# Wider transfers, a gather through SBUF, and the scores of two units as two steps

## The chip, the cores and the metric

The kernel runs on one core of one Trainium2 chip. The metric is the time of one execution in device microseconds (us). The kernel before took 1416.16 us (median of three runs, 1413.11 to 1417.28); lower is better.

## What is computed

The input x has 4 x 1024 tokens of 128 numbers. Four layers follow one another; each works on a normalised copy and adds its result to x (up to constants, as the reference writes them):

```
Q, K, V = h@wq+bq, h@wk+bk, h@wv+bv         # h = norm(x); reshaped to (4*16, 1024, 8)
attn    = softmax(Q K^T / sqrt(8))           # 64 heads, 1024 x 1024 each
y       = norm(attn V reshaped @ wo + bo + h) * gamma + beta
h2      = silu(x@W1) * (x@W2); gelu; gelu    # ternary weights, 128 -> 512 -> 512 -> 512 -> 128
gla     : h = h*exp(g) + k v^T along the sequence; o = q h; gated, projected
moe     : a router picks 3 of 8 zones per batch; gelu(x@Wa[z])@Wb[z], weighted
```

The reshape to (4*16, 1024, 8) takes a head from 64 consecutive tokens over all 128 columns, so Q, K and the result of the attention change their layout between the projection and the scores. The kernel does this through DRAM.

## The kernel before, in words

Tokens are worked on in 8 blocks of 512 (`NBLK`). The attention of a block is 8 heads, taken as 4 pairs, so there are 32 pairs. A pair is 16 units; a unit is 128 keys of one head of the pair against its 1024 queries: two score matmuls (`scores`), one exponential over 128 x 1024 on ScalarE (line 929), and two matmuls with the values (`weigh`, four column groups of 32, line 1466, 8 records for two units). So there are 512 exponentials.

The other layers are cut into small steps that stand between the scores. `class Plan` has a generator for each kind of work (`stream_x` the scores, `stream_l` the loads of pairs, `stream_f` the fetches of results, `stream_q` norm, projection and split of Q and K, `stream_a` the attention's end, `stream_w` weights, `stream_b` the ternary layer, `stream_p`, `stream_r`, `stream_s`, `stream_t` the recurrent layer, `stream_z`, `stream_d` the zones). The string `ORDER` names, letter by letter, which generator takes its next step. Each engine plays its part of this one list strictly in order, with semaphores between engines. SyncE (SP) issues every DMA of the loop, so its queue too is in the order of the list. Unit numbers below are given as pairs: 11.44 is 0.44 of the way through the scores of pair 11.

The steps that matter on SP:

- `keep(b, w, n0, n1)` (line 682) writes the two rounded parts of Q or K of block b to the DRAM tensor QD. A block takes 8 DMAs of 64 KB each for Q and as many for K, in rows of 256 bytes.
- `load_pair(n)` (lines 698 and 707) reads the keys (4 DMAs of 128 KB) and queries (8 DMAs of 32 KB) of a pair into one of three buffers, 786 KB in all. It waits for the kept parts and for the scores of pair n - 3.
- `finish(pr)` (line 760) writes the result of a pair (DVE's copy OS, line 1220) to OD in 4 DMAs, and DVE's next copy waits for them.
- `fetch(pr)` (line 771) reads the numerators and denominators back, 4 DMAs. After four fetches DVE divides (lines 1155 and 1157) and TensorE projects (`project`, line 1478).
- `replica` (line 791) reads one row set of the recurrent layer's values, 16 per block; DVE's `product` (1267) waits for it, its scan (1276) follows.

PSUM has 8 banks. From pair 6 on (`LATE`) banks 0 to 3 are two slots of scores, bank 4 sums the pair's result, banks 5 and 6 are for all other steps in turn (`take`), and bank 7 sums `gather`: four groups of matmuls that pick the outputs of 16 states of a block into one bank, which ScalarE's `heads` then reads. `log_exp`, `tables` and `tanh_with` load another set of function tables on ScalarE (line 901) when the next function isn't in the loaded set; 135 such changes lie in the order.

Of the kernel before, what the change touches and what calls it, by code (L numbers as in the profile page):

```python
# [18 lines left out]
NS = 6  # L19
# [6 lines left out]
    "qqqxwqxxwxxxxwwxxxxxxxxxxxxxwlxxxxxxxxxxxxxwxxxqxxwxxxwxxxxfwxlxxfwxxxxwxxxxlxwxqxwxxxxwlxxxxxfxxxxx"  # L26
    "fawxxxxqwxwxxxxwfxxaxaxxaaxxxxxxwxxxwaxxxwxaxpxxwxwxxxqxwbxlqbbxxqbxxbxbbxxqxbbxxxlqxxxbxlxfbbbbxbfx"
    "lbxxbxbbfxabxbxbxbxxqxabxxxbxaxqxxpaxpxxlrqppxxxxxpxpxxraassaxxxxsrbbxxxqpxssxsxssrxxssxxrxsxsxfrsxx"
    "xsssxsbxxbsrxqxxbrsbsxxrxqslssxxfxsxrssxfxsxbblsxlxbsssxxbbbxrsxbrbxsbrsrbfbxsssxbsbxbbxsxsssabbxxxx"
    "aabxxqxssrraaxxxsqbxsxspsfxxpaxsxxrpqrxxpsqpxpxxaxsxsxsbxpxxsssbxbxsrsxlqxxsxxxrxsxsxsxrsrbbxtbxxlqs"  # L30
    "sssxfbbssxsbrlxrxxtxrtsxqbtsxrxslbbsxsxbxtssbbbxsfssxbssstxxxrbxtxbbxxbxfrasxxsbbssxsxrrsxxslxsaxbss"
    "ssxxsxrrbqsxxxpaxprsxsxsqaxpxxsxpsprpxxsssspxxstssraxxsxqrrxsxftxtaxqxaxsxtrxsbxtsxtbbsbxsfxqssxsbbx"
    "xxsssxxtxbftlrsrbxxsslxxblsxrxbstbbrxsxsfssbbsbqasbsxxbsrxsrxxxxassxasbxxbbxrsxssbaqaxsxtlxbsbrxtxxs"
    "xssfbsxxarbrtxasxxxtbbbbbxspxxxsqxsprxxrpxsxppxttsqxpfsxsssxpsxxbsstrxxsrqsrtxtxxqxsxbxsssxsxxxsbrxs"
    "xxbssssrxbsflxsxbrsbssbbsxbxbrlxlbsxrtsxsbsssxsbbxrrsfsssxtasxbtrxsxssbsxbratsxsxxsxxsbxaxqtxxbrxxxx"
    "aptsxpqsxasxqxxxafprrsqxqxprxsxaxpxxpsxsbxxxssxxsspxsxtfsrlsxxxtxrqbxtbbxstxxssrsxsxrsxtsssbxtxslssr"
    "sbrxslxrsxsfxsrsbxssstxxbsxbslxssxtxbrbxxbbsbxxbrbsrfxxbtsxbssbsxsbrsbtsaxxsbxbxxssaxbxsxxbxarxasplx"
    "xsarstxpxasxxsrpxptfxxxpxpxsrsssxabxxspxfxxstsbxsxxtrssxtxxrxxxrssxsbbxtbsssrtstsxxbsxxxssxtrssrxssr"
    "xxbrfssxsbxxbstxstbxssbsbsbzbfrbbdrdzbtrbsbssassssbsbdrzbbdatdsdadstadsdsbsddbrdsddrtapsdpptssdrazdd"
    "srdpppabdsdsssddbspdbssdddsbrddbrdzbdsdbbrsssbdtsddrdssdststbsbsbssrbbbrbbrstdsssdtbsdrsssbstsstdbsb"  # L40
# [43 lines left out]
class Plan:  # L84
# [57 lines left out]
    def norm_in(self, b):  # L142
        n = self.stats("q", "X", b, ("x_in%d" % b, 16))
        after = [("y_sum", b - 1)] if b >= 2 else []
        return self.apply("q", "XN", "X", b, n, *after)
# [58 lines left out]
    def stream_q(self):  # L204

        for b in range(1, NBLK):
            n = self.stats("q", "X", b, ("x_in%d" % b, 16))
            yield
            after = [("y_sum", b - 1)] if b >= 2 else []
# [199 lines left out]
    def stream_s(self):  # L409


        for n in range(16 * NBLK + 2):
# [8 lines left out]
            if n >= 5 and n % 4 == 1:  # L421
                m = (n - 5) // 4
                assert self.acc >= LATE
                self.add("gather", m // 4, m % 4)
                yield
# [47 lines left out]
x4_in qh gather_ps heads mean_ps rms inv_rms tanh_c swish gate_o scaled_o out_c_ps x3 xt4_ps xt4 pooled route_ps route_act logits_r  # L473
# [3 lines left out]
def build(nc, io, out):  # L477
    ctx = ExitStack()
    with ctx:
# [178 lines left out]
        def _(sp):  # L658
# [19 lines left out]
            def keep(b, w, n0, n1):  # L678
                need.wait_ge("qk_parts", split_no(b, w))
                for n in range(n0, n1):  # L680
                    for i in range(2):
                        sp.dma_start(bass.AP(QD.tensor, QD[w, b, n, i, 0, 0:1].offset, [[64, 16], [2048, 8], [1024, 2], [1, 64]]),  # L682
                                     words(Qp[w][:, i, 128 * n:128 * n + 128])).then_inc(S[kept(b, n, w)], 16)

            def load_pair(n):
                b, i4, k = n // 4, n % 4, n % 3
                need.wait_ge(kept(b, i4, 1), 128 * b + 96 if n else 64)
# [3 lines left out]
                need.wait_ge(kept(b, i4, 0), 128 * b + 96 if n else 64)  # L691
# [29 lines left out]
            def guard(b):  # L721
# [3 lines left out]
                with sp.If_eq(flag, 1):  # L725
                    inner = need.inner()
                    g_dve, g_in = "g_dve%d" % b, "g_in%d" % b
                    for n in range(3):
                        inner.wait_ge("pair_in%d" % ((4 * b + n) % 3), 192 * ((4 * b + n) // 3 + 1))
                    need_kept = ("k_out" if b else "k_out", 128 * b + 96)  # L730
                    inner.wait_ge(*need_kept)
                    inner.wait_ge("q_out", 128 * b + 96)
# [9 lines left out]
                    inner.wait_ge(g_in, 384 + 32)  # L742
# [9 lines left out]
                    inner.wait_ge(g_in, 384 + 32 + 64)  # L752

            def finish(pr):
                b, q = pr // 4, pr % 4
                need.wait_ge("ctx_copied", pr + 1)
                for gg in range(2):
                    for h in range(2):
                        c = 32 * (2 * gg + h)
                        sp.dma_start(bass.AP(OD.tensor, OD[b, q, h, 0, 0, 0, gg, 0:1].offset,  # L760
                                             [[128, 16], [2048, 8], [1, 64]]),
                                     OS[c:c + 16, :]).then_inc(S["ctx_out"], 16)

# [940 lines left out]
```

## Time and profile before

| | us |
|---|---|
| median of three runs | 1416.16 |
| the profiled execution | 1411.4 |
| its span | 1409.6 |
| TensorE busy (mean granted clock 0.862) | 1034.7 |
| ScalarE busy | 885.7 |
| of it the 512 exponentials | 489.8 |
| of it 136 table loads | 174.5 |
| VectorE busy | 686.8 |
| GpSimd busy | 348.6 |

Engines work at the same time, so their times don't add up to the span. Busy shares are averages over two very different stretches: while the attention runs (to about 1147 us) no engine is busy all the time; after it TensorE nearly is.

### The profile page before, as it was taken

The page shows a single profiled execution, that of the slowest core. Times are in us where ns is not written, and L with a number is a line of the kernel's source. Part 1 is how long each engine was busy: PE and PEld are TensorE (multiplying, and loading weights), DVE is VectorE, ACT ScalarE, POOL GpSimd, SP SyncE. Part 2 cuts the span into 40 slices and gives each one's busy share as a digit, 9 for nine tenths or more (in the row PEclk, how much of TensorE's full clock was granted, in tenths as well). Part 3 has the DMA queues.
Part 4 walks back from the last instruction along what each step waited for, and adds up shares of the span by engine and source line. Part 5 has one row for each costly group of instructions (what it writes and reads, how often), then busy time and mean ns, then how long its engine had stood idle before and what let it go on. Part 6 is the DMA issues. An engine that isn't in the chain of part 4 may idle for free.

```text
span 1409.6 us, 16763 instructions
## 1 busy us (share of the span) xinstructions
PE 1034.7 (73%) x5842; PEld 470.4 (33%) x5842; DVE 686.8 (49%) x1235; ACT 885.7 (63%) x1110; POOL 348.6 (25%) x318
## 2 busy tenths in 40 slices
PE   2755588567746956868567977495488789999998
PEld 1211123322223212412233223121152247665666
DVE  3022264053616733656355652763254669979510
ACT  0744579656845955758458876385387876665552
POOL 1000011011302302342223232221132254545300
PEclk7877789878877987998778998797688799999999
DMA  4132112102211222113121221131211123222220
GB/s 106 62 93 78 62 50 61 60 23 69 75 63 40 72 73 69 65 64 79 60 69 53 55 72 65 46 87 56 74 60 58 51 73 97 83 90 98 68 60 16
DMA packets 111423, 93.52 MB, mean 66 GB/s; under 512 B 59184, under 2 KB 82512, under 8 KB 111312
## 3 DMA queue, kind: packets, MB, share of 16 engines
q1 hardware_dynamic: 111168, 92.06, 21.6%
q8 instruction: 67, 1.10, 0.3%
q14 instruction: 44, 0.36, 0.1%
q10 hardware_dynamic: 144, 0.00, 0.0%
HBM read 75.25 MB, written 16.78 MB: 65 GB/s over the span
## 4 chain that ended last, share of the span: by engine, by line
SPq 31%; PE 22%; DMA 16%; DVE 13%; issue 9%; ACT 7%; POOL 3%; ACTq 0%; DVEq 0%; POOLq 0%
SPq L707 15%; DMA R<-VD 10%; SPq L698 6%; PE PS L1466 4%; SPq L682 4%; ACT R L929 4%; PE PS L1626 4%; PE PS L1614 4%; DVE R L1276 3%; PE PS L1443 3%; PE PS L1498 3%; DMA RA<-QD 2%; DVE R L1267 2%; SPq L771 2%; ACT L901 2%
## 5 line engine op out<-in xcount | busy, mean ns | idle before, releaser
L929 ACT ACTIVATE R<-PS 128x1024 f32<-128x1024 f32 x512 | 489.8, 1034 | 248.8 <-PE PS L1443 247.1
L1466 PE MATMUL PS<-R 128*32 128x512 f32 x2048 | 318.4, 669 | 27.4 <-DVE R L1220 27.2
L1443 PE MATMUL PS<-RA 32*128 32x512 f32 x1024 | 186.7, 547 | 137.3 <-DMA RA<-QD 58.3
L882 POOL TENSOR_TENSOR R<-R 128x512 f32<-128x512 f32 x128 | 186.3, 1462 | 301.5 <-ACT R L1004 179.9
L1498 PE MATMUL PS<-RB,WR 128*128 128x512 f32 x640 | 193.3, 443 | 59.0 <-DVE RB L1232 33.4
L1267 DVE TENSOR_TENSOR R<-R 128x512 f32<-128x512 f32 x128 | 103.8, 811 | 262.0 <-DMA R<-VD 257.9
L901 ACT ACT_TABLE_LOAD x136 | 174.5, 1283 | 47.2 <-PE PS L1498 32.1
L1443 PEld LDWEIGHTS PS<-RA 32*128 32x128 f32 x1024 | 72.0, 199 | 380.8 <-ACT R L929 188.1
L1276 DVE TENSOR_TENSOR_SCAN R<-R 128x512 f32<-128x512 f32 x128 | 191.5, 1496 | 2.6
L1498 PEld LDWEIGHTS PS<-RB,WR 128*128 128x128 f32 x640 | 123.5, 202 | 126.9 <-issue 36.1
L868 POOL TENSOR_TENSOR RB<-R,RB 128x512 fp32r<-128x512 f32 x48 | 74.1, 1544 | 278.2 <-DVE RB L1232 257.8
L1626 PEld LDWEIGHTS PS<-R 128*128 128x128 f32 x768 | 97.3, 192 | 38.0 <-issue 35.0
L1053 ACT ACTIVATE R<-PS 128x512 f32<-128x512 f32 x96 | 56.5, 596 | 75.5 <-PE PS L1614 75.4
L1626 PE MATMUL PS<-R 128*128 128x128 f32 x768 | 99.7, 276 | 2.2 <-ACT R L1062 2.0
L1614 PE MATMUL PS<-XT,R 128*128 128x512 f32 x192 | 96.4, 595 | 0.7 <-DMA R<-in_Wb 0.7
L1466 PEld LDWEIGHTS PS<-R 128*32 128x32 f32 x2048 | 48.3, 114 | 133.7 <-issue 90.9
L841 POOL TENSOR_SCALAR rs<-mv 128x4 f32<-128x4 f32 x40 | 15.2, 381 | 268.1 <-DVE mv L1092 260.8
L1570 PE MATMUL PS<-R,hot 128*32 128x512 f32 x256 | 52.5, 677 | 28.0 <-POOL R L882 27.9
L1155 DVE RECIPROCAL R<-R 128x512 f32<-128x512 f32 x8 | 26.7, 3342 | 63.1 <-DMA R<-OD 63.0
L1478 PE MATMUL PS<-wA,R 128*128 128x128 f32 x64 | 11.9, 343 | 58.6 <-DVE R L1284 21.4
L945 ACT ACTIVATE R<-PS,sB 128x512 f32<-128x512 f32 x64 | 42.4, 687 | 18.9 <-PE PS L1498 18.5
L1186 DVE CAST WR<-R 128x512 fp32r<-128x512 f32 x10 | 4.2, 421 | 88.9 <-DMA R<-in_wB 88.9
(121 smaller groups left out, 903.2 us busy)
## 6 DMA issues: line engine op xcount, KB each, us to landing
R<-VD SPq DMA_DIRECT2D x128, 256.0 KB
RA<-QD SPq DMA_DIRECT2D x128, 128.0 KB
QD<-RA SPq DMA_DIRECT2D x128, 64.0 KB, 2.1
RA<-QD SPq DMA_DIRECT2D x256, 32.0 KB
OD<-R SPq DMA_DIRECT2D x128, 32.0 KB, 1.8
R<-OD SPq DMA_DIRECT2D x128, 32.0 KB
R<-in_Wa SPq DMA_DIRECT2D x12, 256.0 KB, 3.5
R<-in_Wb SPq DMA_DIRECT2D x12, 256.0 KB, 4.0
```

What stands on the lines that cost most here:

```text
L698: sp.dma_start(words(KS[k][p:p + 32, :]), bass.AP(QD.tensor, QD[1, n // 4, n % 4, 0, 0, 1024 * gg:1024 * gg + 1].offset, [[0, 2], [2048, 1 ...
L707: sp.dma_start(words(QS[k][p:p + 16, :]), bass.AP(QD.tensor, QD[0, n // 4, n % 4, i, 0, at:at + 1].offset, [[0, 2], [2048, 8], [1, 512]])) ...
L882: pool.tensor_tensor(st, st, Qc, ALU.mult).then_inc(S["qh"], 1)
L901: act.preload_act_table_set(name)
L929: act.activation(PR[u % 4], bank(2 * s, 1024), ACT.Exp, scale=SC).then_inc(S["exp"], 1)
L1267: dve.tensor_tensor(ST[n % NS], ST[n % NS], Kc, ALU.mult).then_inc(S["kv"], 1)
L1276: dve.tensor_tensor_scan(st, Ac, st, CS[:, v:v + 1] if k else 0.0, ALU.mult, ALU.add).then_inc(S["scanned"], 1)
L1443: op = pe.matmul(bank(2 * s + h), exact(KS[k][p:p + 32, 128 * j:128 * j + 128]), exact(QS[k][p:p + 32, :]), start=True, stop=not guarded[0])
L1466: op = pe.matmul(bank(ob)[c:c + 32, :], VAF[b % 2][:, at:at + 32], PR[u % 4][:, 512 * h:512 * h + 512], start=(j == 0), stop=(j == 7), til ...
L1498: return pe.matmul(out_ap, w, x, **kw)
L1614: pe.matmul(bank(bk), WA[r][:, 128 * m:128 * m + 128], xtblock(b), start=True, stop=True).then_inc(S["zone_up_ps"], 1)
L1626: op = pe.matmul(bank(bk)[:, 128 * i:128 * i + 128], HH[t % NH][:, 128 * i:128 * i + 128], WB[r][:, m % 4, :], start=(m == 0 and i == 0), ...
```

## The change

Five edits, of which the first three change transfers:

1. QD and OD are laid out anew. The columns of wq, wk and their biases and the rows of wo are permuted on the host, so that a pair is loaded by two DMAs (keys 512 KB, queries 256 KB) in place of twelve. `keep` writes each part twice: 4 DMAs for a call in place of 2 for each of its pairs; for a whole block 4 of 256 KB in place of 8 of 64 KB, still in rows of 256 bytes.
2. `finish` is one DMA of 128 partitions of 2 KB in place of 4.
3. `fetch` is still 4 DMAs with the same bytes, but now of 64 partitions over two halves of OD, in rows of 256 bytes in place of 512.
4. `gather` takes a bank from the common turn for each of its four groups, and VectorE copies or adds it into a tile GA (in the place of Y2), which `heads` reads. Bank 7 joins banks 5 and 6 in the turn.
5. `stream_x` yields between the scores of unit u and of unit u + 1. ORDER is new: 769 letters x in place of 513, all others in the same number, at other places. The residual's tile Y2 is gone (XN is used), so a norm waits for `x1` and not `y_sum`.

```diff
-    "qqqxwqxxwxxxxwwxxxxxxxxxxxxxwlxxxxxxxxxxxxxwxxxqxxwxxxwxxxxfwxlxxfwxxxxwxxxxlxwxqxwxxxxwlxxxxxfxxxxx"
...
+    "xxxxqxxxxxxqxxxxxxxxxxqxxxxxwxqxxxfxxwxxxxxlxwxxxxxxxxxxxxxxxxxxqxxxxxxxxxxxxxfxxxxxxxxxxxxxxxxwxqxw"
...
-        banks = ((5, 6) if self.acc < 32 else
-                 {"b": (0, 1, 2), "d": (0, 1, 2), "o": (3, 4), "a": (4,), "c": (5, 6)}[who])
+        banks = ((5, 6, 7) if self.acc < 32 else
+                 {"b": (0, 1, 2), "d": (0, 1, 2), "o": (3, 4), "a": (4,), "c": (5, 6, 7)}[who])
...
                 self.add("scores", u)
                 yield
+                self.add("scores", u + 1)
+                yield
...
-                for n in range(n0, n1):
-                    for i in range(2):
-                        sp.dma_start(bass.AP(QD.tensor, QD[w, b, n, i, 0, 0:1].offset, [[64, 16], [2048, 8], [1024, 2], [1, 64]]),
-                                     words(Qp[w][:, i, 128 * n:128 * n + 128])).then_inc(S[kept(b, n, w)], 16)
+                for i in range(2):
+                    for copy in range(2):
+                        at = 2 * copy + i if w else 2 * i + copy
+                        sp.dma_start(bass.AP(QD.tensor, QD[w, b, 2 * n0, at, 0, 0:1].offset,
+                                             [[64, 128], [32768, 2 * (n1 - n0)], [1, 64]]),
+                                     words(Qp[w][:, i, 128 * n0:128 * n1])).then_inc(S[kept(b, n0, w)], 16)
...
             def keys(n, k, landed):
-                for h in range(2):
-                    for gg in range(2):
-                        p = 32 * (2 * h + gg)
-                        sp.dma_start(words(KS[k][p:p + 32, :]),
-                                     bass.AP(QD.tensor, QD[1, n // 4, n % 4, 0, 0, 1024 * gg:1024 * gg + 1].offset,
-                                             [[0, 2], [2048, 16], [1, 1024]])).then_inc(S[landed], 16)
+                sp.dma_start(words(KS[k][:, :]), bass.AP(QD.tensor, QD[1, n // 4, 2 * (n % 4), 0, 0, 0:1].offset,
+                                                         [[0, 2], [1024, 64], [1, 1024]])).then_inc(S[landed], 16)
 
             def queries(n, k, landed):
-                for h in range(2):
-                    for gg in range(2):
-                        for i in range(2):
-                            p, at = 32 * (2 * h + gg) + 16 * i, 1024 * gg + 512 * h
-                            sp.dma_start(words(QS[k][p:p + 16, :]),
-                                         bass.AP(QD.tensor, QD[0, n // 4, n % 4, i, 0, at:at + 1].offset,
-                                                 [[0, 2], [2048, 8], [1, 512]])).then_inc(S[landed], 16)
+                sp.dma_start(words(QS[k][:, :]), bass.AP(QD.tensor, QD[0, n // 4, 2 * (n % 4), 0, 0, 0:1].offset,
+                                                         [[512, 2], [1024, 64], [1, 512]])).then_inc(S[landed], 16)
...
             def finish(pr):
...
-                for gg in range(2):
-                    for h in range(2):
-                        c = 32 * (2 * gg + h)
-                        sp.dma_start(bass.AP(OD.tensor, OD[b, q, h, 0, 0, 0, gg, 0:1].offset,
-                                             [[128, 16], [2048, 8], [1, 64]]),
-                                     OS[c:c + 16, :]).then_inc(S["ctx_out"], 16)
+                sp.dma_start(OD[b, q, :, :], OS).then_inc(S["ctx_out"], 16)
 
             def fetch(pr):
...
-                for h in range(2):
-                    for n, dst in enumerate((CT, DT)):
-                        sp.dma_start(dst[b % 2][64 * h:64 * h + 64, 128 * q:128 * q + 128],
-                                     bass.AP(OD.tensor, OD[b, q, h, 0, n, 0, 0, 0:1].offset,
-                                             [[2048, 8], [128, 8], [1, 128]])).then_inc(S["ctx_in%d" % (b % 2)], 16)
+                for n, dst in enumerate((CT, DT)):
+                    for gg in range(2):
+                        at = 128 * q + 64 * gg
+                        sp.dma_start(dst[b % 2][:, at:at + 64],
+                                     bass.AP(OD.tensor, OD[b, q, 64 * gg + 8 * n, 0:1].offset,
+                                             [[16384, 2], [64, 64], [1, 64]])).then_inc(S["ctx_in%d" % (b % 2)], 16)
...
+            def gather(b, q, bk, added):
+                need.wait_ge("gather_ps", 4 * b + q + 1)
+                if q == 0:
+                    if b:
+                        need.wait_ge("heads", b)
+                    dve.tensor_copy(GA, bank(bk)).then_inc(S["gathered"], 1)
+                else:
+                    need.wait_ge("gathered", 4 * b + q)
+                    dve.tensor_tensor(GA, bank(bk), GA, ALU.add).then_inc(S["gathered"], 1)
```

## Rows read from the trace of the kernel before

**Rows 1.** The page's chain of work that ended last, shares of the span.

```profile
SPq 31%; PE 22%; DMA 16%; DVE 13%; issue 9%; ACT 7%; POOL 3%; ACTq 0%; DVEq 0%; POOLq 0%
SPq L707 15%; DMA R<-VD 10%; SPq L698 6%; PE PS L1466 4%; SPq L682 4%; ACT R L929 4%; PE PS L1626 4%; PE PS L1614 4%; DVE R L1276 3%; PE PS L1443 3%; PE PS L1498 3%; DMA RA<-QD 2%; DVE R L1267 2%; SPq L771 2%; ACT L901 2%
```

**Rows 2.** Windows: stretch, length, busy time of five engines, PEclk, DMA share, GB/s.

```profile
194.00:1147.00 953.00, 676.76 (x3816) 267.30 (x3811) 473.07 (x861) 652.69 (x777) 242.18 (x212) 0.84 0.20 62
1147.00:1409.60 262.60, 250.37 (x1365) 170.23 (x1363) 161.85 (x242) 141.52 (x235) 95.93 (x82) 1.00 0.24 74
```

**Rows 3.** Windows of pair loads (408), keeps (76, 342) and replicas (424), same columns.

```profile
408.00:418.00 10.00, 3.02 (x19) 1.14 (x17) 0.00 (x0) 4.60 (x6) 0.00 (x0) 0.88 0.13 51
76.00:81.00 5.00, 1.06 (x12) 0.30 (x4) 1.81 (x3) 3.27 (x4) 0.00 (x0) 1.00 0.63 145
342.00:348.00 6.00, 5.31 (x40) 1.46 (x34) 4.68 (x5) 5.99 (x9) 3.95 (x2) 1.00 0.40 85
424.00:430.00 6.00, 0.00 (x0) 0.00 (x0) 0.56 (x1) 0.00 (x0) 0.00 (x0) 0.50 0.39 126
```

**Rows 4.** Single lines: count, shortest/median/longest in ns, first and last start.

```profile
L707 SPq DMA_DIRECT2D RA<-QD x256: 593/1038/3077, 24.0 to 1079.6; - x128
L698 SPq DMA_DIRECT2D RA<-QD x128: 593/638/3422, 21.1 to 1073.9; - x128
L682 SPq DMA_DIRECT2D QD<-RA x128: 537/617/2207, 14.6 to 940.9; - x128
L760 SPq DMA_DIRECT2D OD<-R x128: 308/437/1797, 86.5 to 1152.3; - x128
L771 SPq DMA_DIRECT2D R<-OD x128: 577/577/1673, 109.3 to 1157.2; - x128
```

**Rows 5.** Timeline of SP around the start of pair 8: start, us, what.

```profile
231.13 2.61 SPq L698 DMA_DIRECT2D RA<-QD  x4
233.79 6.17 SPq L707 DMA_DIRECT2D RA<-QD  x8
240.00 5.06 SPq L698 DMA_DIRECT2D RA<-QD  x4
245.10 11.05 SPq L707 DMA_DIRECT2D RA<-QD  x8
...
265.08 7.75 SPq L707 DMA_DIRECT2D RA<-QD  x8
273.87 2.42 SPq L760 DMA_DIRECT2D OD<-R  x4
283.37 2.58 SPq L771 DMA_DIRECT2D R<-OD  x4
```

**Rows 6.** Timeline just after, with the idle time before each and its releaser.

```profile
287.65 3.35 DVE L1155 RECIPROCAL R<-R 128x512 f32<-128x512 f32 x1 [35.58 <-DMA R<-OD]
291.79 2.08 PE L1478 MATMUL PS<-wA,R 128*128 128x128 f32 x8 [19.07 <-DVE R L1157]
```

**Rows 7.** The same view at pair 12.

```profile
429.44 0.69 DVE L1267 TENSOR_TENSOR R<-R 128x512 f32<-128x512 f32 x1 [25.49 <-DMA R<-VD]
430.52 0.79 PE L1498 MATMUL PS<-RB,WR 128*128 128x512 f32 x1 [19.50 <-DVE RB L1232]
```

**Rows 8.** Costliest groups: count, busy us, mean ns, idle before and its releaser.

```profile
L929 ACT ACTIVATE R<-PS 128x1024 f32<-128x1024 f32 x512 | 489.8, 1034 | 248.8 <-PE PS L1443 247.1
L901 ACT ACT_TABLE_LOAD x136 | 174.5, 1283 | 47.2 <-PE PS L1498 32.1
L1443 PE MATMUL PS<-RA 32*128 32x512 f32 x1024 | 186.7, 547 | 137.3 <-DMA RA<-QD 58.3 <-ACT R L929 56.4 <-issue 19.8
L1498 PE MATMUL PS<-RB,WR 128*128 128x512 f32 x640 | 193.3, 443 | 59.0 <-DVE RB L1232 33.4 <-DVE R L1243 6.7 <-DVE R L1284 5.2
L1220 DVE COPY R<-PS 128x512 f32<-128x512 f32 x32 | 21.9, 683 | 20.0 <-PE PS L1466 19.6 <-issue 0.3
L1267 DVE TENSOR_TENSOR R<-R 128x512 f32<-128x512 f32 x128 | 103.8, 811 | 262.0 <-DMA R<-VD 257.9
```

More of the change, by code:

```diff
@@ L31 @@
[L31 to L40, printed above, removed]
@@ L143, in norm_in @@
         n = self.stats("q", "X", b, ("x_in%d" % b, 16))
-        after = [("y_sum", b - 1)] if b >= 2 else []
+        after = [("x1", b - 1)] if b >= 2 else []
         return self.apply("q", "XN", "X", b, n, *after)
@@ L208, in stream_q @@
             yield
-            after = [("y_sum", b - 1)] if b >= 2 else []
+            after = [("x1", b - 1)] if b >= 2 else []
             e = self.apply("q", "XN", "X", b, n, *after)
@@ L422, in stream_s @@
                 m = (n - 5) // 4
-                assert self.acc >= LATE
-                self.add("gather", m // 4, m % 4)
+                self.add("gather", m // 4, m % 4, self.take("c"), self.count("gathered"))
                 yield
@@ L920, in attend, with scores @@
                 need.wait_ge("va", 1)
-            def scores(u0):
-                log_exp()
-                for u in (u0, u0 + 1):
-                    pr, j, gg, b, g, s = unit(u)
-                    need.wait_ge("scores", u + 1)
-                    if u >= 4:
-                        need.wait_ge("pv", u - 3)
-                    act.activation(PR[u % 4], bank(2 * s, 1024), ACT.Exp, scale=SC).then_inc(S["exp"], 1)
+            def scores(u):
+                pr, j, gg, b, g, s = unit(u)
+                need.wait_ge("scores", u + 1)
+                if u >= 4:
+                    need.wait_ge("pv", u - 3)
+                log_exp()
+                act.activation(PR[u % 4], bank(2 * s, 1024), ACT.Exp, scale=SC).then_inc(S["exp"], 1)
             def ternary_begin():
@@ L1170, in residual @@
                 for op, i in ((ALU.mult, 1), (ALU.add, 2)):
[L1171 removed]
+                    own.step(dve.tensor_tensor(XN[b % 2], XN[b % 2], bc(i), op))
                     own.settle()
[L1173 removed]
+                dve.tensor_tensor(xblock(b), xblock(b), XN[b % 2], ALU.add).then_inc(S["x1"], 1)
             def turn(b, bk, e):
@@ L1433, in scores @@
                 k, n = pr % 3, pr % 4
-                need.wait_ge("pair_in%d" % k, 192 * (pr // 3 + 1))
+                need.wait_ge("pair_in%d" % k, 32 * (pr // 3 + 1))
                 if guarded[0]:
                     need.wait_ge("ones", 18)
-                slots = [(unit(u + gg)[5], gg) for gg in range(2)]
-                for s, gg in slots:
-                    for h in range(2):
-                        room(2 * s + h)
-                    for h in range(2):
-                        p = 32 * (2 * h + gg)
-                        op = pe.matmul(bank(2 * s + h), exact(KS[k][p:p + 32, 128 * j:128 * j + 128]),
-                                  exact(QS[k][p:p + 32, :]), start=True, stop=not guarded[0])
-                        emptied[2 * s + h] = ("exp", u + gg + 1)
-                    if not guarded[0]:
-                        op.then_inc(S["scores"], 1)
-                for s, gg in slots if guarded[0] else ():
-                    for h in range(2):
-                        p = 32 * (2 * h + gg)
-                        op = pe.matmul(bank(2 * s + h), view(GSEL[p:p + 8, n:n + 1], (0, 128)), exact(GQ[p:p + 8, :]),
-                                       start=False, stop=True)
-                    op.then_inc(S["scores"], 1)
+                for h in range(2):
+                    room(2 * s + h)
+                for h in range(2):
+                    p = 32 * (2 * h + gg)
+                    op = pe.matmul(bank(2 * s + h), exact(KS[k][p:p + 32, 128 * j:128 * j + 128]),
+                                   exact(QS[k][p:p + 32, :]), start=True, stop=not guarded[0])
+                    emptied[2 * s + h] = ("exp", u + 1)
+                for h in range(2) if guarded[0] else ():
+                    p = 32 * (2 * h + gg)
+                    op = pe.matmul(bank(2 * s + h), view(GSEL[p:p + 8, n:n + 1], (0, 128)), exact(GQ[p:p + 8, :]),
+                                   start=False, stop=True)
+                op.then_inc(S["scores"], 1)
             def weigh(u):
@@ L1562, in proj_c, with gather @@
                 emptied[bk] = freed
-            def gather(b, q):
-                if q == 0:
-                    room(7)
+            def gather(b, q, bk, added):
+                room(bk)
                 for i in range(4):
@@ L1569, in gather @@
                     need.wait_ge("qh", n + 1)
-                    op = pe.matmul(bank(7)[32 * i:32 * i + 32, :], hot[:, q, :], ST[n % NS], start=(q == 0), stop=(q == 3),
+                    op = pe.matmul(bank(bk)[32 * i:32 * i + 32, :], hot[:, q, :], ST[n % NS], start=True, stop=True,
                                    tile_position=(0, 32 * i))
                 op.then_inc(S["gather_ps"], 1)
-                emptied[7] = ("heads", b + 1)
+                emptied[bk] = added
             def mean_mm(b, bk):
```

94 lines of the change are left out of this document (53 added, 41 removed).

## The prediction

> **What bounds the kernel now.** I read the chain of waits first [rows 1]. No engine leads it: SP's own queue makes 31% of it and transfers 16%, together 47%, and the largest single line is the issue of the query loads (L707, 15%), with that of the key loads (L698) 6%. Next the windows [rows 2]. From 1147 us on TensorE is busy 250.4 of 262.6 us at a granted clock of 1.00: that tail is bound by TensorE. From 194 to 1147 us ScalarE is busy 652.7 of 953 (0.68) and TensorE 676.8: neither is full, so here the waits decide. Over these 26 pairs ScalarE works 652.7/26 = 25 us a pair, which I take as a pair's length where nothing stalls.
>
> What stalls is seen in the timeline at a block's start. SP issues the loads of pairs 8, 9 and 10 from 231.1 to 272.8, and only then the writes of pair 7's result (273.9), which land late, so that the fetch starts at 283.4 [rows 5]. DVE divides at 287.7 after 35.6 us of idle time, TensorE projects at 291.8 after 19.1 us [rows 6]. At pair 12 it is a replica that is stuck behind the loads: DVE waited 25.5 us for it and TensorE 19.5 us for DVE [rows 7].
>
> Why do the loads take so long? While only they run, the DMA share is 0.13, which is 2 of 16 engines, at 51 GB/s [rows 3]. A pair is 786 KB, so 15.4 us, and three in a row are 46 us, which is what SP took (41.7, with the last still moving). An issue's shortest time is 0.59 us and the median of L707 1.04 [rows 4]: SP waits for room in the queue. The loads' bytes on two engines, not the number of instructions, set the time. The source's leading dimension is 2. Replicas have a leading 8 and show 0.39 (6.2 engines, gaps included), keeps have 16 or 128 and reach 0.63 [rows 3].
>
> **The change part by part.** The sum starts from the profiled execution, 1411.4 us, which is 4.8 under the median of the runs.
>
> *Loads, two issues for twelve.* Bytes and leading dimension (2) stay, so I take 15.4 us a pair as now; the ten issues fewer are hidden in the queue's own time. If they weren't, they would be worth 32 x 10 x 0.59 = 189 us at most; I take 0. By the Trainium skill (DMA: Bandwidth & Descriptors, Rules for kernel authors) a leading dimension below 16, a zero-stride copy above all, confines a DMA to that many engines; the trace agrees for the old form (0.13 of 16). By its advice to coalesce small transfers (same section) the merging should have gained; the rule on engines speaks against it here.
>
> *Where loads stand.* I walked both orders and looked at how far TensorE must get from a block's projection to the loads of the next block that stand back to back, in pairs: before 2.88, 2.37, 2.50, 3.13, 2.88 for blocks 3 to 7 and 3.06 to the end; after 2.94, 2.62, 2.75, 2.68, 3.25 and 2.94. That is 0.36 more, +9 us at 25. In two blocks (pairs 12 to 14 and 28 to 30) one load is now issued earlier and leaves the group: 2 x 15.4 = -31.
>
> *Keeps.* A window of keeps moves 85 GB/s at a share of 0.40, so 13.3 GB/s for one engine in rows of 256 bytes; the 4096-byte rows of the loads reach 51/2.08 = 24.5 [rows 3]. A part was 8 issues x 0.62 = 4.9 us of SP [rows 4]. It is now 1.05 MB over 16 engines, 1.05/0.213 = 4.9 us. Nothing changes on SP, but two keeps stand now directly before the loads (blocks 4 and 6): +10.
>
> *Fetches.* Each was 4 x 0.58 = 2.3 us of issue [rows 4]. With a leading 2 and 256-byte rows I take 131 KB on two engines at 13.3 GB/s: 4.9 us. On the path to the division in 7 blocks: 7 x 2.6 = +18. In the groups of loads stand five fetches (24.5 us) where four stood (10.3): +14. From below: if they ran as wide as now, 0.
>
> *Finish.* 4 issues (1.75 us) become one (0.44): 7 x 1.3 = -9. TensorE, DVE and the fetch wait for it.
>
> *Tables.* Counted in both orders, 105 changes of table instead of 135; up to the last `weigh` 77 instead of 111. 34 x 1.283 us [rows 8] = 43.6 us of ScalarE; of it 0.68 counts, ScalarE's busy share: -30. The four more in the tail are hidden, ScalarE works 142 of 263 us there.
>
> *Gather on DVE.* 32 more operations on a full bank, 32 x 0.683 (the copy L1220, [rows 8]) = 22 us. DVE is busy 473 of 953 us [rows 2] and these wait for nothing late: 0 (bounds 0 and +22).
>
> *Scores in two steps, and bank 7.* No instruction is added. TensorE waited 56.4 us for ScalarE ahead of scores [rows 8]; other work may now fill that, and a third bank lets it run ahead. Bounds 0 and -56; most of this wait lies beside exponentials that bound the pair anyway, so -12.
>
> *The tail.* It takes over one `hid_mm`, four `gate_mm`, two gathers and one projection: 8 + 16 matmuls at 0.30 (193.3/640, [rows 8]), the rest at about 0.3 too, 24 x 0.3 + 9 x 0.3 = +10 on a full TensorE. Seven more products and scans (0.81 us the product) are hidden on DVE, 162 of 263.
>
> Sum: -31 + 9 + 10 + 18 + 14 - 9 - 30 - 12 + 10 = -21: 1390 for the profiled execution; 1395 would be the same against the median, I take 1392.
>
> **The rivals.**
>
> *Two engines get fuller: slower.* The engines that carry the loads carry everything else too. Per pair in us: load 15.4; four replicas of 262 KB over 8 engines, 4 x 1.34 = 5.4; fetch 0.9; keep 1.2; finish 0.6: 23.5. After: 15.4, 5.4, 4.9, 2.3 and 0.7: 28.7, or +5.2, x 29 pairs = 151 us. If what is queued behind them waits longer in step (DVE already waits 257.9 us for replicas, [rows 8]) and the 47% of the chain that is SP and transfers holds, this costs 71 us; less the 42 of it counted above (keeps and fetches), +29 on 1390 without the -31 (groups of loads don't help when the engines are full): 1450. It decides once these two engines are busy over about 0.8 of the attention's time; now they are at 23.5/36.7 (953/26) = 0.64. That speaks for it half.
>
> *The planned places are right and more is won.* Stalls at the block starts shrink by more than I count, since pair 12's load now stands 1 pair earlier and pair 15's too. Pair 12 waited some 30 us; one such stall gone in three of six blocks with the tables: 1300.
>
> *Loads spread.* If the merged loads ran on 16 engines, or SP were free after issue, the 21% of the chain in L707 and L698 (296 us) would shrink by 259 (64 issues of about 0.6 stay): near 1150. Nothing in the rows speaks for it but the chain.
>
> *It doesn't do what it says.* The scores' second step is worth nothing, since `weigh` still follows both; then the rest cancels: 1412, no change.
>
> **How the numbers follow.** Forecast (small gain) 0.40, its own range 1350 to 1415; full engines, 1450, 0.33; better places, 1300, 0.12; loads spread, 0.07; no change 0.08. About 0.3% (4 us) is what can be told from no change. Faster: 0.34 of the forecast, 0.12, 0.07 = 0.53; same 0.09; slower 0.38. The range 1290 to 1470 leaves out the spread loads and the ends of the others.
>
> **What would show it.** Right: windows with only pair loads still at 0.13 of the DMA engines and about 51 GB/s; query loads that occupy SP for some 10 us each, keys less; fetches of over 1 us an issue; table loads near 106; the tail from the last `weigh` at 270 us or so. Wrong: a share near 1.0 in the loads, or SP free between them; DVE's wait for replicas far above 258 us would be the slower case. The prediction falls if the attention ends before 1090 or after 1180 us.

## The result and the profile after

The changed kernel takes 1428.45 us (median of 4 runs, 1426.18 to 1430.38), the kernel before 1414.63 in the same comparison: ratio 1.0101, interval 1.0076 to 1.0126. It is slower by 1.0%; 1392, a gain, was forecast. The time lies inside the range, the sign is the other one. The profiled execution has a span of 1426.2 us, 16.6 more than before.

The chain of waits, by engine and by line, answers to [rows 1]:

```profile
DMA 27%; SPq 23%; PE 22%; DVE 14%; issue 7%; ACT 5%; POOL 2%; DVEq 0%; ACTq 0%; POOLq 0%
DMA R<-VD 10%; SPq L762 9%; DMA OD<-R 6%; PE PS L1461 5%; DMA RA<-QD 5%; PE PS L1441 4%; SPq L704 3%; SPq L686 3%; ACT R L919 3%; PE PS L1608 3%; PE PS L1620 2%; DVE R L1266 2%; SPq L782 2%; PE PS L1493 2%; DVE R L1257 2%
```

SP's share went from 31 to 23%, that of the transfers from 16 to 27%. The load lines (L704 and L700, before L707 and L698) have nearly left the chain, the fetches (L762) head SP's part with 9%. SP and transfers together are 50% where they were 47%: the waiting changed its name.

Windows, columns as in [rows 2] and [rows 3]: the attention from pair 6 on, the tail after the last exponential, and a stretch with only pair loads.

```profile
199.00:1134.95 935.95, 683.38 (x3784) 277.14 (x3780) 446.79 (x847) 606.61 (x733) 227.95 (x202) 0.84 0.23 72
1134.95:1426.20 291.25, 267.25 (x1404) 177.32 (x1402) 199.18 (x292) 152.85 (x250) 119.93 (x92) 0.99 0.24 74
50.00:61.00 11.00, 10.06 (x72) 2.73 (x64) 0.69 (x1) 10.75 (x12) 0.00 (x0) 0.97 0.13 52
```

The last exponential ends at 1134.95 us (before at 1146.5): the attention gained 11.6 us. The tail takes 291.3 us (before 263.1): it lost 28.2. In the tail TensorE works 267.3 instead of 250.8 us and is idle for 24.0 instead of 12.2. While loads run, 0.13 of the engines move 52 GB/s, as before [rows 3].

Single lines, as [rows 4]; L704 and L700 are the loads, L686 the keeps, L752 the finish, L762 the fetches, L782 the replicas:

```profile
L704 SPq DMA_DIRECT2D RA<-QD x32: 490/825/12565, 26.2 to 1077.5; - x32
L700 SPq DMA_DIRECT2D RA<-QD x32: 484/813/11698, 25.5 to 1076.9; - x32
L686 SPq DMA_DIRECT2D QD<-RA x80: 359/620/7809, 15.1 to 989.1; - x80
L752 SPq DMA_DIRECT2D OD<-R x32: 320/422/9092, 85.4 to 1136.8; - x32
L762 SPq DMA_DIRECT2D R<-OD x128: 485/951/10428, 88.8 to 1152.7; - x128
L782 SPq DMA_DIRECT2D R<-VD x128: 574/591/12311, 323.3 to 1336.3; - x128
```

The medians of the loads are 0.8 us, but every line now has a longest issue of 8 to 13 us. The first two or three large DMAs go into the queue at once, and whatever SP issues next pays. All fetch issues together took 249.5 us (before 81.6), all replica issues 144.6 (88.7), the 64 loads 138.9 (before 358.3 for 384). SP's sum is 725 us against 720: nothing was saved.

The timeline of SP at the start of pair 8, as [rows 5], and what followed, as [rows 6]:

```profile
247.25 1.02 SPq L700 DMA_DIRECT2D RA<-QD  x1
251.77 0.50 SPq L704 DMA_DIRECT2D RA<-QD  x1
252.32 6.21 SPq L700 DMA_DIRECT2D RA<-QD  x1
258.56 5.06 SPq L704 DMA_DIRECT2D RA<-QD  x1
263.67 10.05 SPq L700 DMA_DIRECT2D RA<-QD  x1
273.76 5.22 SPq L704 DMA_DIRECT2D RA<-QD  x1
279.99 8.89 SPq L752 DMA_DIRECT2D OD<-R  x1
298.71 2.98 SPq L762 DMA_DIRECT2D R<-OD  x4
```

```profile
305.00 3.35 DVE L1145 RECIPROCAL R<-R 128x512 f32<-128x512 f32 x1 [34.48 <-DMA R<-OD]
309.13 2.08 PE L1473 MATMUL PS<-wA,R 128*128 128x128 f32 x8 [19.26 <-DVE R L1147]
```

From the first load to the projection it is 309.1 - 247.3 = 61.9 us, before 291.8 - 231.1 = 60.7. One write of the result (L752) holds SP for 8.9 us, where four took 2.4: it stands behind the loads. So the one write for four saves little: all 32 took 49.3 us of issue, before 59.9 for 128.

Costliest groups, as [rows 8]:

```profile
L919 ACT ACTIVATE R<-PS 128x1024 f32<-128x1024 f32 x512 | 492.5, 1032 | 272.3 <-PE PS L1441 269.4
L892 ACT ACT_TABLE_LOAD x106 | 136.0, 1283 | 82.1 <-PE PS L1493 43.6 <-PE PS L1572 17.0 <-PE PS L1441 13.7
L1441 PE MATMUL PS<-RA 32*128 32x512 f32 x1024 | 213.6, 541 | 116.0 <-DMA RA<-QD 77.5 <-ACT R L919 26.5 <-issue 9.2
L1257 DVE TENSOR_TENSOR R<-R 128x512 f32<-128x512 f32 x128 | 102.7, 802 | 220.4 <-DMA R<-VD 213.4 <-ACT R L975 6.8
```

30 table loads fewer, 38.5 us of ScalarE; ScalarE nevertheless waits longer for scores (269.4 us against 247.1).

### The profile page after: what moved, and what is told of

The parts are those of the page before. It is cut to its first block, busy times and chain, and to the rows that moved or that the text cites. A ratio compares the mean times of both kernels' runs of the same rounds, so it can differ in the third digit from the quotient of the medians.

```text
span 1426.2 us, 16361 instructions
## 1 busy us (share of the span) xinstructions
PE 1059.6 (74%) x5842; PEld 486.3 (34%) x5842; DVE 693.5 (49%) x1267; ACT 851.0 (60%) x1080; POOL 356.5 (25%) x318
## 4 chain that ended last, share of the span: by engine, by line
DMA 27%; SPq 23%; PE 22%; DVE 14%; issue 7%; ACT 5%; POOL 2%; DVEq 0%; ACTq 0%; POOLq 0%
DMA R<-VD 10%; SPq L762 9%; DMA OD<-R 6%; PE PS L1461 5%; DMA RA<-QD 5%; PE PS L1441 4%; SPq L704 3%; SPq L686 3%; ACT R L919 3%; PE PS L1608 3%; PE PS L1620 2%; DVE R L1266 2%; SPq L782 2%; PE PS L1493 2%; DVE R L1257 2%
## 5 line engine op out<-in xcount | busy, mean ns | idle before, releaser
L919 ACT ACTIVATE R<-PS 128x1024 f32<-128x1024 f32 x512 | 492.5, 1032 | 272.3 <-PE PS L1441 269.4
L1461 PE MATMUL PS<-R 128*32 128x512 f32 x2048 | 322.7, 680 | 69.2 <-DVE R L1210 69.2
L1441 PE MATMUL PS<-RA 32*128 32x512 f32 x1024 | 213.6, 541 | 116.0 <-DMA RA<-QD 77.5
L873 POOL TENSOR_TENSOR R<-R 128x512 f32<-128x512 f32 x128 | 189.6, 1489 | 296.1 <-ACT R L994 186.5
L1441 PEld LDWEIGHTS PS<-RA 32*128 32x128 f32 x1024 | 82.8, 198 | 388.9 <-ACT R L919 180.1
L1257 DVE TENSOR_TENSOR R<-R 128x512 f32<-128x512 f32 x128 | 102.7, 802 | 220.4 <-DMA R<-VD 213.4
L1266 DVE TENSOR_TENSOR_SCAN R<-R 128x512 f32<-128x512 f32 x128 | 185.9, 1453 | 2.9
L892 ACT ACT_TABLE_LOAD x106 | 136.0, 1283 | 82.1 <-PE PS L1493 43.6
L1493 PEld LDWEIGHTS PS<-RB,WR 128*128 128x128 f32 x640 | 127.0, 206 | 102.5 <-issue 30.4
L859 POOL TENSOR_TENSOR RB<-R,RB 128x512 fp32r<-128x512 f32 x48 | 70.1, 1463 | 177.2 <-DVE RB L1222 156.9
L832 POOL TENSOR_SCALAR rs<-mv 128x4 f32<-128x4 f32 x40 | 19.2, 480 | 375.0 <-DVE mv L1082 359.5
L1145 DVE RECIPROCAL R<-R 128x512 f32<-128x512 f32 x8 | 26.8, 3352 | 70.0 <-DMA R<-OD 70.0
L1210 DVE COPY R<-PS 128x512 f32<-128x512 f32 x32 | 21.9, 683 | 71.7 <-PE PS L1461 69.0
L983 ACT ACTIVATE R<-X,nm,rs 128x128 f32<-128x128 f32 x64 | 26.3, 486 | 50.4 <-POOL nm L841 50.4
```

The costliest lines, as they stand in the source:

```text
L859: pool.tensor_tensor(part(tile(dst)[:, 1, :]), whole(src), part(tile(dst)[:, 0, :]), ALU.subtract).then_inc(S["lo_pool"], 1)
L873: pool.tensor_tensor(st, st, Qc, ALU.mult).then_inc(S["qh"], 1)
L892: act.preload_act_table_set(name)
L919: act.activation(PR[u % 4], bank(2 * s, 1024), ACT.Exp, scale=SC).then_inc(S["exp"], 1)
L1257: dve.tensor_tensor(ST[n % NS], ST[n % NS], Kc, ALU.mult).then_inc(S["kv"], 1)
L1266: dve.tensor_tensor_scan(st, Ac, st, CS[:, v:v + 1] if k else 0.0, ALU.mult, ALU.add).then_inc(S["scanned"], 1)
```

## Experiments

In all of them "attention" is the time to the end of the last exponential and "tail" the rest of the span, both of the profiled execution. Before: 1146.5 and 263.1. After: 1135.0 and 291.3. One profiled execution can lie some 5 us off its kernel's median (a1: 1391.16 against 1385.81), so smaller differences of attention or tail say little by themselves.

### Which half of the change costs

`a1_old_transfers`: the changed kernel with `keep`, `keys`, `queries`, `finish`, `fetch`, the layouts QD and OD, their semaphore counts and the unpermuted weights of before.

> The changed kernel with the layouts and transfers of before (12 loads a pair, 8 keeps, 4 finishes, fetches of 512-byte rows); new order, gather through SBUF, three common banks and split scores stay. Theory 1 (the new transfers cost, since fetches are confined to two engines and keeps are doubled; the new order by itself gains in the attention and loses in the tail): 1390 to 1412, the last exponential before 1125 us, the tail still about 290. Rival 2 (the transfers are neutral, the new order, gather and split are the loss): 1422 to 1435, as the changed kernel.

`a2_transfers_alone` is the reverse: the kernel before with exactly those parts from the changed one.

> The kernel before with the new layouts and transfers alone; old order, old gather, scores together. Theory 1: 1430 to 1450, the last exponential some 20 to 30 us later than 1147, the tail at 263 as before. Rival 2: 1410 to 1418, no change. If merging the loads were worth SP's freed time: below 1380.

Measured: a1 1385.81 us, ratio to before 0.9815 (0.9790 to 0.9840); a2 1444.87 us, ratio 1.0245 (1.0229 to 1.0260). The windows of attention and tail, first of a1, then of a2:

```profile
0.00:1096.93 1096.93, 788.45 (x4440) 308.36 (x4440) 493.89 (x975) 697.83 (x831) 234.58 (x226) 0.84 0.22 66
1096.93:1389.20 292.27, 267.47 (x1404) 177.32 (x1402) 199.41 (x292) 152.76 (x250) 120.09 (x92) 0.99 0.25 74
```

```profile
0.00:1176.95 1176.95, 792.92 (x4473) 301.42 (x4474) 520.59 (x992) 743.52 (x875) 252.17 (x236) 0.81 0.24 73
1176.95:1441.00 264.05, 253.35 (x1370) 172.06 (x1369) 163.12 (x244) 142.11 (x235) 98.55 (x83) 0.99 0.24 74
```

The transfers cost in the attention and only there: a2 is 30.5 us later than before, and the changed kernel 38.0 later than a1. The order (with gather, split and the residual's tile) gains 49.6 us in the attention (a1 against before) and costs 29.2 in the tail; the tail is the same with either set of transfers. Theory 1 stands, the rival falls; a1's time came 4 us below the range given for it, a2's lies inside.

### What the transfers' width is worth

`a3_wide_loads`: two DMAs of 64 partitions for the keys, two for the queries, leading dimension 64; the bytes, the order and the place of each row stay.

```diff
-                sp.dma_start(words(KS[k][:, :]), bass.AP(QD.tensor, QD[1, ...].offset,
-                                                         [[0, 2], [1024, 64], [1, 1024]]))
+                for h in range(2):
+                    sp.dma_start(words(KS[k][64 * h:64 * h + 64, :]),
+                                 bass.AP(QD.tensor, QD[1, ...].offset, [[1024, 64], [1, 1024]]))
```

> The changed kernel with each pair's keys and queries as two DMAs each of 64 partitions, the leading dimension 64 in place of 2; bytes and order the same. Two-engine theory (786 KB on 2 of 16 engines take 15.4 us and hold back what is queued behind): while loads run the DMA share goes from 0.13 to over 0.4, a pair lands in 2 to 4 us, the attention shrinks by 100 to 250 us: 1180 to 1330. Rival (SP's issues or the compute engines bound the attention, the transfers only fill gaps): 1400 to 1428.

Measured 1144.34 us, ratio 0.8114 (0.8095 to 0.8132). A window of loads (with keeps beside them), attention and tail:

```profile
33.00:41.00 8.00, 7.22 (x38) 1.64 (x36) 0.00 (x0) 6.73 (x8) 0.00 (x0) 0.61 0.91 218
0.00:849.11 849.11, 743.77 (x4440) 293.00 (x4440) 502.32 (x975) 694.75 (x831) 233.35 (x226) 0.94 0.38 99
849.11:1142.20 293.09, 268.65 (x1404) 178.18 (x1402) 199.82 (x292) 152.90 (x250) 119.64 (x92) 0.99 0.25 74
```

The DMA share is 0.91 where it was 0.13, the attention ends at 849.1 us, 285.8 earlier, and the tail hasn't moved. That is more than the 100 to 250 us expected. The issues are twice as many, 128 for 64, and took less of SP: 83.9 us for 138.9. ScalarE's wait ahead of its exponentials fell to a third:

```profile
L923 ACT ACTIVATE R<-PS 128x1024 f32<-128x1024 f32 x512 | 490.5, 1037 | 92.0 <-PE PS L1445 89.6
```

`e1_wide_fetch_alone` cuts only the fetches in halves (`for h in range(2)`, partitions 64h to 64h + 64, `[[64, 64], [1, 64]]`); the loads stay narrow. (A DMA of the changed fetch fills 128 partitions, 64 from each half of OD: that is its leading 2.)

> The changed kernel with each fetch as 8 DMAs of 64 partitions (leading dimension 64) in place of 4 with a leading 2; loads still on two engines. If the fetches on two engines are most of what the new transfers cost (+34 us): 1395 to 1410. If the doubled keeps are: 1420 to 1428. If the fetches mostly wait behind the loads on engines that both use, widening them changes little: within 6 us of 1428.

Measured 1401.32 us, ratio 0.9918 (0.9892 to 0.9944), less than before. Attention and tail:

```profile
0.00:1107.14 1107.14, 782.50 (x4440) 305.32 (x4440) 494.37 (x975) 698.15 (x831) 234.92 (x226) 0.84 0.25 76
1107.14:1399.10 291.96, 268.50 (x1404) 178.14 (x1402) 197.24 (x292) 153.06 (x250) 118.76 (x92) 0.99 0.25 74
```

The attention is 27.8 us shorter than the changed kernel's. So the fetches are most of what the transfers cost; keeps and the rest are left with about 10 of 38 us. VectorE's wait for the fetch itself (ahead of L1145) fell from 70.0 to 61.4 us and its wait for replicas from 213.4 to 194.2: more of the cost lay in what stood behind the fetches than in the fetches.

`a4_wide_both` has both edits.

> As the one with wide loads, and each fetch too as 64 partitions with a leading dimension of 64 (8 DMAs in place of 4). If a fetch on two engines is worth its computed 4.9 us on the path of 7 blocks: 10 to 30 us less than with wide loads alone. Rival: once the loads no longer fill those engines the fetch is hidden or its 4 extra issues (2.3 us a pair on SP) cost as much: within 5 us, or slower.

Measured 1142.45 us, ratio 0.8080 (0.8051 to 0.8109): not to be told from wide loads alone, as the rival had it. VectorE's wait for the fetch was 29.9 us in a3 and is 28.7 here, so the narrow fetch cost next to nothing once the loads no longer filled two engines; its issues took 160.1 us of SP in place of 140.4.

`i1_before_wide_24` leaves order and layouts of before and cuts its loads along the leading 2: 24 issues a pair in place of 12, of 16 and 8 partitions.

> The kernel before, layouts, order and bytes unchanged, with each load of a pair cut along its leading 2 so that keys go as 8 DMAs of 16 partitions and queries as 16 DMAs of 8: 24 issues a pair in place of 12, 16 and 8 engines wide in place of 2. If the two engines are what bounds the attention: issues of 0.59 us make 14.2 us of SP a pair, nearly the 15.4 us of now, but nothing waits behind full engines: 1220 to 1340. If SP's time is the bound in either form: 1390 to 1430.

Measured 1256.12 us, ratio 0.8888 (0.8851 to 0.8925); attention 992.5, tail 263.1. Twice the issues with the same bytes are 11% faster: the old kernel too was held by the two engines and not by the number of issues. Its 768 load issues even took less of SP than the 384 of before, 271.5 us for 358.3. The 113 us between it and a4 are those issues (SPq is still 24% of its chain), the layouts and the new order together; the next run parts the order from the rest.

### Whether the new order is better without the stalls

`b1_before_wide_both`: the kernel before with the new layouts and wide loads and fetches.

> The old order, old gather and scores together, with the new layouts and wide loads and fetches (leading 64). Against the same transfers in the new order (1142): if the new order is the better one only where stalls hide its longer tail, this one is within 10 us or faster, its tail at 263; if its 30 fewer table loads (38 us of ScalarE) count in full once the stalls are gone, this one is 20 to 45 us slower: 1162 to 1187.

Measured 1173.02 us, ratio 0.8296 (0.8252 to 0.8340), 31 us more than a4, as the second case had it, and 83 less than i1, which has the same order. Attention and tail:

```profile
0.00:908.58 908.58, 753.88 (x4478) 290.01 (x4479) 526.90 (x994) 742.77 (x875) 254.94 (x237) 0.91 0.37 95
908.58:1172.50 263.92, 252.28 (x1366) 171.89 (x1364) 161.99 (x242) 142.38 (x235) 98.44 (x82) 0.99 0.24 74
```

Against a4 (851.6 and 291.7) the old order loses 57.0 us in the attention and wins 27.8 in the tail. ScalarE's work in the attention is 742.8 against 694.8 us: the 48 us less, mostly 34 table loads (43.6), would account for most of the 57 if all of it counts.

### The tail

`d1_short_scans` leaves out most of the recurrence: the scans of the last 46 states run over 64 of 512 tokens.

```diff
-                dve.tensor_tensor_scan(st, Ac, st, ...
+                m = 64 if n >= 82 else 512
+                dve.tensor_tensor_scan(st[:, 0:m], Ac[:, 0:m], st[:, 0:m], ...
```

> The changed kernel with the scans of the last 46 states (those of the tail) over 64 of 512 tokens, so it leaves out most of the recurrence there; nothing else. It takes about 46 x 1.2 = 55 us of VectorE's 199 out of the tail. Theory 1 (VectorE sets the pace of the tail from 1180 to 1280): the tail falls from 291 to between 270 and 282, near TensorE's own 267, and TensorE's idle time in it from 24 towards 12 us. Rival (TensorE's waits in the tail have another cause): the tail stays within 3 us of 291.

`d2_before_short_scans` does the same to the last 39 states of the kernel before (`n >= 89`).

> The control of the run with short scans: the kernel before, with the scans of the last 39 states (those of its tail) over 64 of 512 tokens, so it too leaves out most of the recurrence there. It takes 39 x 1.2 = 47 us of VectorE's 162 out of a tail of 263 us in which TensorE is busy 250. If the old tail is bound by TensorE and only the new one by the scans: the tail falls by 3 to 8 us, to 255 to 260, and what is left between the two short-scan tails (273 and this) is the 17 us of TensorE's moved work. If scans set the pace of both tails: below 252.

Measured: d1 1408.03 us, ratio 0.9965 (0.9945 to 0.9986); d2 1402.50 (two runs), ratio 0.9920 (0.9891 to 0.9949). The tails, d1 first:

```profile
1130.48:1403.50 273.02, 258.95 (x1404) 176.48 (x1402) 146.74 (x292) 152.52 (x250) 98.65 (x92) 0.99 0.26 79
```

```profile
1144.03:1400.60 256.57, 248.86 (x1369) 171.55 (x1368) 121.57 (x243) 141.76 (x235) 90.10 (x82) 0.99 0.25 76
```

The new tail falls by 18.3 us (291.3 to 273.0), the old one by 6.5 (263.1 to 256.6). So about 11.8 of the 28.2 us go with the recurrence on VectorE, and 16.4 stay. That the untouched kernels differ by 267.3 - 250.8 = 16.5 us of TensorE's busy time doesn't explain those 16.4: with short scans TensorE's busy time differs by 259.0 - 248.9 = 10.1 only, and its idle time by the other 6.3 (14.1 against 7.7). The busy time itself had grown with the waiting. The gather's matmuls, in the tails of before, d2, after and d1, have the same mean time, but the same number covers less time where the scans are short:

```profile
L1570 PE MATMUL PS<-R,hot 128*32 128x512 f32 x88 | 16.0, 605 | 2.1 <-POOL R L882 2.1
L1571 PE MATMUL PS<-R,hot 128*32 128x512 f32 x88 | 13.5, 605 | 0.0
L1564 PE MATMUL PS<-R,hot 128*32 128x512 f32 x104 | 21.3, 605 | 2.9 <-POOL R L873 2.9
L1565 PE MATMUL PS<-R,hot 128*32 128x512 f32 x104 | 14.9, 605 | 0.0
```

Of the 6.3 us of idle time most falls into the first 40 us of the tail: TensorE is idle for 4.5 us there in the changed kernel and in d1, for 1.5 in the kernel before and 0.7 in d2. No run tests its cause.

Windows of the tail show the waiting for VectorE too, first of before, then of after:

```profile
1180.00:1230.00 50.00, 48.25 (x242) 31.94 (x241) 45.10 (x60) 33.78 (x57) 28.25 (x21) 1.00 0.31 90
1230.00:1280.00 50.00, 47.98 (x264) 32.00 (x263) 38.55 (x60) 34.56 (x63) 25.01 (x23) 1.00 0.25 83
```

```profile
1180.00:1230.00 50.00, 45.25 (x245) 29.38 (x244) 46.46 (x78) 23.41 (x40) 30.65 (x27) 1.00 0.21 64
1230.00:1280.00 50.00, 46.32 (x241) 31.04 (x240) 49.27 (x60) 32.38 (x60) 31.34 (x24) 1.00 0.26 85
```

VectorE (third busy number) works 49.3 of 50 us from 1230 to 1280, before 38.6, and TensorE 46.3 where it had 48.0 (in d1 50.0). The chain through 1180 to 1300 us, of the changed kernel, of d1 and of the kernel before:

```profile
by line: issue 15.1%; DVE R L1266 12.5%; DMA R<-VD 12.4%; DVE R L1257 10.5%; PE PS L1608 5.4%; PE PS L1620 4.6%; DVE R L1091 4.2%; POOL rs L834 4.1%; POOL R L873 4.0%; DVE RB L1222 3.7%; DVE stats L1076 2.7%; PE PS L1564 2.5%; PE PS L1493 2
```

```profile
by line: PE PS L1609 23.5%; PE PS L1621 23.1%; PE PS L1494 14.3%; DMA R<-VD 8.0%; PE PS L1565 6.8%; PE PS L1556 5.9%; PE PS L1534 4.7%; DVE R L1267 1.8%; DVE RB L1222 1.7%; issue 1.7%; PE PS L1580 1.7%; PE PS L1573 1.4%; DVE RB L1227 1.4%; 
```

```profile
by line: DMA R<-VD 12.6%; DVE R L1276 11.8%; PE PS L1614 10.9%; DVE R L1267 9.0%; issue 8.4%; PE PS L1626 7.7%; PE PS L1570 5.9%; PE PS L1498 4.8%; DVE R L1101 2.6%; PE PS L1560 2.5%; POOL rs L843 2.3%; DVE RB L1237 1.9%; POOL rs L841 1.8%;
```

Scan (L1266) and product (L1257) make 23% of the first, the replica that the product waits for 12%; in the second TensorE's zone matmuls (L1609, L1621) head with 47% and the scan (L1267 there) is left with 1.8%. In the third, of the kernel before, scan and product (L1276, L1267) have 21% and the zone matmuls 19, against 10 in the first. So the old chain ran through the recurrence too, with TensorE close behind it: idle for 3.8 us from 1180 to 1280, in the changed kernel for 8.4, in d1 for 1.0. That fits with short scans winning 6.5 us there and 18.3 here; the chain alone wouldn't have told.

### Gather and split

`c1_gather_in_psum` takes back the gather: groups summed in bank 7, no VectorE operations, two common banks.

> The changed kernel with the old gather: four groups summed in bank 7, read there by ScalarE, no copies or adds on VectorE, two common banks. Theory 1 (the tail is longer because VectorE, busy 49 of 50 us from 1230 to 1280, got more to do; the 13 gather operations of 0.68 us in it are 9 us of that): tail 291 falls to about 280 to 284, the attention stays within 5 us of 1135; in all 1416 to 1424. Rival (the tail's 28 us are TensorE's own moved work and its waits): no change, 1425 to 1431. If the third bank is what helps the attention: slower, over 1435.

`c2_scores_together` moves, in ORDER, the second x of every round directly behind the first (129 of 256 rounds had something between them).

> The changed kernel with each score step of unit u + 1 moved directly behind that of unit u (129 of the 256 rounds have something between them); all else in the new order. If the split is worth the 12 us that I took in the prediction: 1435 to 1445. If it is worth nothing, since weigh still follows both: 1424 to 1432. If steps between the scores hold ScalarE up: faster, below 1422.

Measured: c1 1430.25 us, ratio 1.0128 (1.0106 to 1.0151), attention 1135.4, tail 293.0; c2 1422.24, ratio 1.0062 (1.0040 to 1.0083), attention 1129.6, tail 293.1. The gather and the third bank together are worth nothing that can be measured: c1 takes 7 us of VectorE's work out of the tail (199.2 to 192.1), and the tail stays, as its rival had it. Theory 1 of that run, VectorE's sum as the pace, gets no support. But c1 changes three things at once, and they may offset each other: with one bank for all four groups TensorE waits 3.0 us ahead of the gather in the tail for ScalarE to read that bank, and it has one common bank fewer. That product and scan count and the adds don't is therefore likely, not shown.

c2's time lies between its second case (from 1424) and its third (below 1422). The split gains nothing here and, if anything, costs 0.4% (the intervals 1.0040 to 1.0083 and 1.0076 to 1.0126 barely touch). Nor is the split all that c2 takes back: the moved letters also leave two table loads fewer, 104 for 106, 2.6 us of ScalarE.

`h1_wide_both_together` is a4 with the scores side by side again.

> The changed kernel with wide loads and fetches and the two score steps of a round side by side again. With narrow loads that was 6 us faster than the split. If the steps between the scores delay ScalarE's next exponential: 3 to 10 us faster than 1142. If with short stalls the split finally fills TensorE's wait for ScalarE (26 us in 250 places): slower, 1145 to 1160.

Measured 1152.28 us, ratio 0.8154 (0.8121 to 0.8187), against 0.8080 (0.8051 to 0.8109) with the split. With short stalls the split is worth about 10 us, nearly the 12 that I had forecast for it in the kernel with long ones: the first case of the expectation falls. The waits differ too. With long stalls the split cuts TensorE's wait for ScalarE ahead of scores from 34.6 to 26.5 us, but ScalarE's wait for scores grows from 220.0 to 269.4; with short ones it cuts the first from 32.2 to 25.7 and leaves the second at 85.2 and 86.6. Why the second wait grows only with long stalls isn't tested.

## Why the prediction was wrong, step by step

In us of the profiled executions, forecast against what the runs showed:

| step | forecast | shown | by |
|---|---|---|---|
| loads, keeps, fetches, finish | +33 | +30.5 / +38.0 | a2 - before / after - a1 |
| of it fetches | +32 | +27.8 | after - e1 |
| of it keeps, finish, loads | +1 | about +10 | the rest of after - a1 |
| places of the loads and tables | -52 | about -55 | the order's -49.6 less the split's 5.3 |
| scores in two steps, bank 7 | -12 | +5.3, 0 | c2, c1 (attention) |
| tail: TensorE's moved work | +10 | +10.1 | busy time, d1 - d2 |
| tail: products and scans | 0 | +11.8 | what goes with short scans |
| tail: other waits of TensorE | none | +6.3 | idle time, d1 - d2 |
| sum | -21 | +16.6 | |

**What bounds the kernel** was right. Loads stayed on two engines (0.13, 52 GB/s), a3 took 286 us off by their width alone and i1 showed it for the old layout. The rule of the Trainium skill that I weighed (DMA: Bandwidth & Descriptors, Rules for kernel authors: a leading dimension below 16 confines a DMA to at most that many engines) agrees with both forms here: 0.13 with a leading 2, 0.91 with 64. Another line of that section of the Trainium skill says of two transfers to disjoint partition halves "Don't bother", because both halves use all 16 engines anyway, and advises one transfer of 128 partitions. Its reason doesn't hold for the transfer here: the one of 128 partitions, with a leading 2, ran at 0.13, and its two halves took 0.20 off the ratio.

**Loads, two issues for twelve: 0** was right, but not by all of its reason. I said that a query load would hold SP for some 10 us. The median is 0.8: the queue takes some large DMAs whole, and the next fetch, write or replica waits in their place. The sum over all issues came out alike (725 against 720 us); that the two engines set it is what a3 and i1 speak for.

**Fetches** were right in size: the sum of the two terms, 32, against 27.8. The way there was other than I had it: 18 of the 32 lay on the path to the division, but VectorE's wait for the fetch moved by 8.6 us between e1 and the changed kernel and its wait for replicas by 19.2.

**Keeps and finish** were too small: +10 and -9 against about +10 together. The finish's gain isn't seen, since the single write also stands behind the loads (8.9 us at pair 8); no run parts the two.

**Places and tables** were right in sum, as far as a remainder shows it. That 0.68 is the share of ScalarE's saved work that counts wasn't tested by itself, nor were the places (+9 and -31).

**Scores in two steps and bank 7** failed: the -12 was a guess between 0 and -56, and the measured sign is the other one. The 56 us in which TensorE waits for ScalarE are beside the exponentials, and these are behind transfers. The reasoning that such waits are hidden spoke for 0, and I took -12 all the same. c2 and h1 show on what it hangs: +5.3 us of attention with long stalls, at the edge of what can be told, and about -10 of time without them.

**The tail** is the step that failed by most: "seven more products and scans are hidden on DVE, 162 of 263". That is a mean over a stretch of which the last 60 us hold none of this work; in the 50 us from 1230 on VectorE had 49.3 to do. The term that I put at 0 was worth 11.8 us, as d1 and d2 show. TensorE's moved work was rightly +10: its busy time differs by 10.1 us where the scans don't hold it up. I did count a gather's four matmuls as four records where the trace has two for each (104 against 88 for two gathers more), but that miscount cost little. Another 6.3 us are waits of TensorE that stay with short scans; the sum has no term for them, and their cause stays open. The two misses, 17 us of split and 18 of tail, are 35 of the 38 us between -21 and +16.6.

**The rival that is slower** (full engines, 1450) had the sign, and the fetches on the two engines as its place, but not the size: the forecast of the transfers alone, +33, was near the 30.5 to 38.0 shown, and the extra 29 us did not come. Its own sign, a wait for replicas far above 258 us, isn't there either: that wait fell to 213.4. a2, where nothing makes up for the transfers, took 1444.87. The stated signs of the forecast were met by the share of 0.13, the 106 table loads and the end of the attention; not by the query loads (median 0.8 us for some 10) and the tail (291 us for 270).

## What to carry to other kernels

Before DMAs are merged, read the share of engines while only they run: 0.13 is two of sixteen, and in this kernel what helped was to cut the DMAs along that leading 2. a4 (1142.45 us) beats the kernel before by 19% and the changed one by 20% with a loop over two halves. When an order of steps moves work into another stage, look at that stage's fullest window and at how far the next engine stands behind the chain; a stage's mean hides both. And a busy time can hold waiting: compare it with a run in which the wait is gone before it is called work.

## What was not expected of the hardware

- Queue room: two loads of 512 and 256 KB on two engines are issued in about 1.1 us (25.5 to 26.7 us and 118.1 to 119.2); what is issued next then stands: four fetches from 120.5 take 17.0 us together. With 12 small DMAs the loads themselves had waited (L707: median 1.04 us, shortest 0.59).
- A scan over 64 instead of 512 columns in 46 of 128 states, some 52 us of VectorE's work, takes 18.3 us off the new tail; for 39 states it takes 6.5 off the old one, where TensorE stands closer behind.
- Busy time of TensorE: the same 104 records of the gather's matmuls, at the same mean of 605 ns, cover 21.3 us in the changed kernel and 14.9 with short scans.
- The granted clock was higher where the stalls were shorter: mean 0.859 for the changed kernel, 0.952 with wide loads, at the same matmuls.
